# Expert rows through a padded buffer, scattered during attention, instead of a routing table and gathers

## The reference, cut to what matters

```python
xf = layernorm(x).reshape(T, d)                      # T = 2048, d = 256
probs = jax.nn.sigmoid(xf @ gate_w.T)
top_vals, sel = jax.lax.top_k(probs, 2)
weights = top_vals / (top_vals.sum(-1, keepdims=True) + 1e-06)
ranks = (position of each choice among the choices of its expert)
valid = ranks < capacity                             # 320
slot = jnp.where(valid, flat_sel * capacity + ranks, sentinel)
padded = jnp.zeros((sentinel + 1, d)).at[slot].set(x_rep)
h = jax.nn.gelu(einsum('ecd,edf->ecf', padded, w1))
out_padded = einsum('ecf,efd->ecd', h, w2)
out = sum over the two choices of weights * out_padded[slot]
x = x + tanh(g_ffn) * out
```

## Time and profile before

| | us |
|---|---|
| median of 3 runs | 384.05 |
| the profiled execution | 383.44 |
| its span, first to last instruction | 381.7 |
| busy in the span: PE, DVE, ACT, POOL | 315.4, 238.7, 198.0, 243.6 |
| mean granted TensorE clock | 0.933 of 2.4 GHz |

### The profile page before, as it was taken

The page is one execution under the profiler, slowest core; times in us unless marked ns, Lnnn a source line. Parts: engine busy times, 40 slices in busy tenths (PEclk is TensorE's granted clock), DMA queues, the critical chain, the costliest instruction groups (busy, mean ns, idle before and its releaser), DMA issues.

```text
span 381.7 us, 7062 instructions
## 1 busy us (share of the span) xinstructions
PE 315.4 (83%) x2140; PEld 282.1 (74%) x2140; DVE 238.7 (63%) x611; ACT 198.0 (52%) x565; POOL 243.6 (64%) x306
## 2 busy tenths in 40 slices
PE   3989989999999999978402999999999888989500
PEld 2677868988889898867301999999998888879500
DVE  1275968678999898987871476666555535476000
ACT  1073687787876778662510465655645555453100
POOL 6323466755758585655436458888888878787562
PEclk9999999999999999999855799999999999999955
DMA  7794000001011000101106247877776667664332
GB/s 216 231 314 140 2 2 14 29 33 39 27 37 35 27 27 27 41 25 49 42 16 217 64 153 203 209 187 185 200 172 140 145 132 171 172 122 50 41 40 29
DMA packets 31800, 38.23 MB, mean 100 GB/s; under 512 B 4624, under 2 KB 25760, under 8 KB 31776
## 3 DMA queue, kind: packets, MB, share of 16 engines
q1 hardware_dynamic: 23808, 27.44, 22.4%
q0 software_dynamic: 7936, 10.49, 16.8%
q10 hardware_dynamic: 32, 0.02, 0.0%
HBM read 28.10 MB, written 9.83 MB: 99 GB/s over the span
## 4 chain that ended last, share of the span: by engine, by line
POOL 16%; PE 14%; DMA 10%; issue 8%; DVE 2%; ACT 1%; ACTq 0%; POOLq 0%; DVEq 0%
POOL out_dram L551 11%; DMA out_dram<-wqT,rows_to 8%; PE ps_scores L1197 6%; POOL xg L539 4%; PE ps_out L1213 4%; DMA xg<-z_rows,rows_from 2%; PE ps_pT L1181 2%; PE ps_misc L1213 1%; POOL payload L474 0%; ACT wqT L698 0%; PE ps_scores L1115 0%; DVE value_t L963 0%; DVE gden L931 0%; ACT value_t L663 0%; DVE top_i L866 0%
## 5 line engine op out<-in xcount | busy, mean ns | idle before, releaser
L551 POOL DMA_INDIRECT out_dram<-wqT,rows_to x48 | 82.6, 1721 | 24.0 <-issue 11.9
L1197 PE MATMUL ps_scores<-value_t,score_t 128*128 128x320 f32 x384 | 61.1, 316 | 5.8 <-DVE value_t L963 5.8
L539 POOL DMA_INDIRECT xg<-z_rows,rows_from x48 | 49.2, 1025 | 23.5 <-issue 13.4
L1197 PEld LDWEIGHTS ps_scores<-value_t,score_t 128*128 128x128 f32 x384 | 57.8, 192 | 7.1 <-DVE value_t L963 4.7
L1095 PE MATMUL ps_scores<-score_t,xn 128*128 128x512 f32 x192 | 54.4, 426 | 0.0
L1129 PE MATMUL ps_out<-value_t,pT 128*128 128x256 f32 (+1 forms) x384 | 54.0, 291 | 0.4 <-DVE x L840 0.2
L970 DVE TENSOR_TENSOR score_t<-raw,score_t 128x1024 fp32r<-128x1024 f32 x16 | 19.6, 1224 | 51.7 <-ACT score_t L670 33.1
L1129 PEld LDWEIGHTS ps_out<-value_t,pT 128*128 128x128 f32 x384 | 48.7, 193 | 1.2 <-DVE x L840 0.9
L1213 PE MATMUL ps_out<-score_t,value_t 128*128 128x256 f32 x336 | 43.9, 287 | 0.0
L1213 PEld LDWEIGHTS ps_out<-score_t,value_t 128*128 128x128 f32 x336 | 41.0, 191 | 0.9
L1095 PEld LDWEIGHTS ps_scores<-score_t,xn 128*128 128x128 f32 x192 | 36.3, 189 | 6.9
(11 more groups left out here) (171 smaller groups left out, 632.2 us busy)
## 6 DMA issues: line engine op xcount, KB each, us to landing
raw<-in_L_ffn_w_dram SPq DMA_DIRECT2D x32, 512.0 KB
out_dram<-x SPq DMA_DIRECT2D x16, 128.0 KB, 1.7
z_rows<-z SPq DMA_DIRECT2D x16, 128.0 KB, 1.7
x_all<-in_x_dram SPq DMA_DIRECT2D x1, 1536.0 KB, 9.7
wkv_a<-in_L_xattn_Wkv_dram SPq DMA_DIRECT2D x2, 512.0 KB, 7.8
wq_sb<-in_L_xattn_Wq_dram SPq DMA_DIRECT2D x1, 1024.0 KB, 8.8
wo_sb<-in_L_xattn_Wo_dram SPq DMA_DIRECT2D x1, 1024.0 KB, 13.3
xg<-z_rows,rows_from POOLq DMA_INDIRECT x48
```

What stands on the lines that cost most here:

```text
L539: pool.indirect_dma_start(xg[0:SLOTS[k], j, k], None, z2_rows, bass.IndirectOffsetOnAxis(ap=rows_from[0:SLOTS[k], at:at + 1], axis=0)).the ...
L551: pool.indirect_dma_start(out, bass.IndirectOffsetOnAxis(ap=rows_to[0:SLOTS[k], at:at + 1], axis=0), y[0:SLOTS[k], j, k], None, compute_op ...
L1197: op = pe.matmul(ps_scores[:, f, 0:CAPACITY], w1_hl(p, a)[:, c, f * P:(f + 1) * P], x_hl(p, b)[:, c], start=c == 0 and (a, b) == PARTS[0], ...
```

## The change

Rows go from SBUF into a padded buffer in DRAM, `padded`, 2048 rows for each expert, 258 numbers each: the row, its token, its weight. SP fills the first 320 rows of each expert with zeros, with weight 0 and with the spare tokens. Each pair's rows are scattered during attention, two indirect DMAs in each step, four for a pair, to row 2048 x expert + rank. An expert's rows are then fetched by two plain DMAs, and POOL reads token and weight out of what was fetched (`mark`). The table, `z2_rows` and the gathers go; both loops are written out.

```diff
-    z2_rows = nc.dram_tensor("z2_rows", [TOKENS, DIM], F32, kind="Internal").ap()
+    padded = nc.dram_tensor("padded", [EXPERTS * TOKENS, ROW], F32, kind="Internal").ap()
+    padded_init = padded.rearrange("(e s) r -> s e r", e=EXPERTS)
...
-            with engine.Fori(FIRST, LAST) as i:
-                for count, per in counts:
-                    count.enter(i, FIRST, per)
-                for j in range(2):
-                    step(i * 2 + j, j, i)
...
         @block.sync
...
+            sp.wait_ge(empty_ready, 1)
+            for k in range(SLOT_TILES):
+                n = SLOTS[k]
+                sp.dma_start(padded_init[k * P:k * P + n], empty[0:n, k, None, :].to_broadcast([n, EXPERTS, ROW])
+                             ).then_inc(empty_stored, 16)
...
-                t = s - 4
-                if exists(t):
-                    sp.wait_ge(z2_ready, t + 1)
-                    sp.dma_start(z2_rows[bass.ds(t * P, P), :], z2[:, j]).then_inc(z2_stored[j], 16)
...
+            steps(step)
+            for k in range(2):
+                sp.wait_ge(dispatched[k], 64 * PAIRS // 2)
+
+            def fetch(e):
+
+                if exists(e, EXPERTS):
+                    wait(sp, xg_turned, e - 1)
+                    wait(sp, marked, e - 1)
+                    at = e * TOKENS
+                    sp.dma_start(xg[:, e % 2, 0:2], padded[at:at + 2 * P, :].rearrange("(k p) r -> p k r", p=P)
+                                 ).then_inc(fetched[e % 2], 16)
+                    sp.dma_start(xg[0:SLOTS[2], e % 2, 2], padded[at + 2 * P:at + CAPACITY, :]).then_inc(fetched[e % 2], 16)
+
+            fetch(0)
+            fetch(1)
...
                 if exists(e, EXPERTS - 2):
                     sp.wait_ge(w1_low, e + 1)
+                    sp.dma_start(raw1[:, j], w1_load[e + 2]).then_inc(w_loaded[j], 16)
                     sp.wait_ge(w2_low, e + 1)
+                    sp.dma_start(raw2[:, j], w2_load[e + 2]).then_inc(w_loaded[j], 16)
+                if e >= -2:
+                    fetch(e + 4)
...
         @block.gpsimd
...
+            def dispatch(r, k):
+
+                for q in range(2):
+                    pool.indirect_dma_start(padded, bass.IndirectOffsetOnAxis(ap=slot_row[:, r % 2, k, q:q + 1], axis=0),
+                                            z2[:, 2 * (r % 2) + k, q], None).then_inc(dispatched[r % 2], 16)
...
-                    pool.tensor_tensor(payload[:, :, :, :], at_c[:, :, None, :].to_broadcast([P, 4, 3, COLS]),
...
+                if exists(r, PAIRS) and r < PAIRS - 1:
+                    if j == 0:
+                        mark_tokens(r)
+                        pool.wait_ge(slots_ready, r + 1)
+                        if r == 0:
+                            pool.wait_ge(empty_stored, 16 * SLOT_TILES)
+                    dispatch(r, j)
...
-                        done.carry(pool_scratch, minus)
...
-                    done.done(pool.tensor_tensor(l2[:, p, 2:3], l2[:, p, 1:2], mv2[:, p, 0:1], ALU.mult))
-                    pool.tensor_tensor(l2[:, p, 3:4], l2[:, p, 2:3], minus[:, :], ALU.mult).then_inc(ln2_ready, 1)
+                    pool.tensor_scalar(l2[:, p, 2:3], mv2[:, p, 0:1], l2[:, p, 1:2], -1.0, ALU.mult, ALU.mult).then_inc(ln2_ready, 1)
...
+            def mark(e):
+
+                if exists(e, EXPERTS):
+                    pool.wait_ge(fetched[e % 2], 32 * (e // 2 + 1))
+                    done.mark(pool.tensor_scalar(rows_to[:, e], xg[:, e % 2, :, TOKEN], 0.0, None, ALU.add))
+                    pool.tensor_scalar(slot_w[:, e], xg[:, e % 2, :, WEIGHT], 0.0, None, ALU.add).then_inc(marked, 1)
+
+            for e in range(2):
+                mark(e)
+            for e in range(EXPERTS):
                 j, i = e % 2, e // 2
...
-                        pool.indirect_dma_start(xg[0:SLOTS[k], j, k], None, z2_rows,
-                                                bass.IndirectOffsetOnAxis(ap=rows_from[0:SLOTS[k], at:at + 1], axis=0)
-                                                ).then_inc(gathered[j][k], 16)
...
+                mark(e + 2)
+                done.sync()
+                wait(pool, added[(j + 1) % 2], SLOT_TILES * 16 * (i + j))
...
-                    act.activation(z2[:, p], x1[:, p], ACT.Identity, bias=l2[:, p, 3:4],
-                                   scale=l2[:, p, 1:2]).then_inc(z2_ready, 1)
+                    if t >= RING:
+                        act.wait_ge(dispatched[t // 2 % 2], 64 * (t // RING))
+                    act.activation(z2[:, t % RING, :, 0:DIM], x1[:, p, None, :].to_broadcast([P, 2, DIM]), ACT.Identity,
+                                   bias=l2[:, p, 2:3], scale=l2[:, p, 1:2]).then_inc(z2_ready, 1)
...
+                    act.wait_ge(marked, e + 1)
...
+                    if r >= 2:
+                        dve.wait_ge(dispatched[r % 2], 64 * (r // 2))
+                    dve.scalar_tensor_tensor(slot_row[:, r % 2], ef[:, :, :], float(TOKENS), rank[:, :, :], ALU.mult, ALU.add
+                                             ).then_inc(slots_ready, 1)
...
-                        for n in range(4):
-                            op = pe.matmul(ps_table, at_p[:, n], payload[:, n].rearrange("p m c -> p (m c)"),
-                                           start=n == 0, stop=n == 3)
-                        op.then_inc(tabled, 1)
```

More of the change, by code:

```diff
@@ L74, in sync @@
     def sync(self):
[L76 to L90, removed]
+        wait(self.engine, self.sem, self.k)
 def exists(t, n=TILES):
-    return not isinstance(t, int) or 0 <= t < n
-def upto(t, n=TILES):
-    return min(t, n) if isinstance(t, int) else t
+    return 0 <= t < n
 def wait(engine, sem, value):
-    if not isinstance(value, int) or value > 0:
+    if value > 0:
         engine.wait_ge(sem, value)
 def build(nc, x, ctx_in, mask, g_xattn, g_ffn, ln_gamma, ln_beta, wq, wkv, wo, bo, gate_w, w1, w2, out):
-    z2_rows = nc.dram_tensor("z2_rows", [TOKENS, DIM], F32, kind="Internal").ap()
+    padded = nc.dram_tensor("padded", [EXPERTS * TOKENS, ROW], F32, kind="Internal").ap()
+    padded_init = padded.rearrange("(e s) r -> s e r", e=EXPERTS)
     x_rows = x.rearrange("b (t p) d -> (b t) p d", p=P)
@@ L297, in build @@
         w1_high, w1_low, w2_high, w2_low = (sem(n) for n in ("w1_high", "w1_low", "w2_high", "w2_low"))
-        gathered = [[sem(f"gathered{p}_{k}") for k in range(SLOT_TILES)] for p in range(2)]
+        fetched = [sem(f"fetched{k}") for k in range(2)]
+        marked = sem("marked")
         added = [sem(f"added{k}") for k in range(2)]
@@ L337, in steps, with expert_steps @@
                         job(n, *JOBS[n])
-            with engine.Fori(FIRST, LAST) as i:
-                for count, per in counts:
-                    count.enter(i, FIRST, per)
-                for j in range(2):
-                    step(i * 2 + j, j, i)
[L343 to L360, removed]
+        def expert_steps(step):
+            for e in range(-4, EXPERTS):
                 step(e, e % 2, e // 2)
@@ L651, in step @@
                     op.then_inc(exped1, 1)
-            steps(act, step, job=job, jobs_after={-1: range(N_FIRST, N_KEYS + 4), 0: JOBS_AFTER[0]})
+            steps(step, job=job, jobs_after={-1: range(N_FIRST, N_KEYS + 4), 0: JOBS_AFTER[0]})
             act.wait_ge(gated, TILES)
@@ L866, in step @@
                         link.mark(dve.max_index(top_i[:, k], top[:, k], prob[:, k]))
-                if place:
-                    link.sync()
-                    link.mark(dve.scalar_tensor_tensor(over2[:, :, :], rank[:, :, :], float(2 * P), over1[:, :, :], ALU.is_ge, ALU.add))
-                    link.mark(dve.scalar_tensor_tensor(slot_b[:, :, :], ef[:, :, :], float(SLOT_TILES), invalid[:, :, :], ALU.mult, ALU.add))
                 if exists(t1):
@@ L891, in step @@
                     link.sync()
-                    link.mark(dve.scalar_tensor_tensor(slot_p[:, :, :], over2[:, :, :], -float(P), rank[:, :, :], ALU.mult, ALU.add))
-                    link.mark(dve.tensor_tensor(slot_c[:, :, :], slot_b[:, :, :], over2[:, :, :], ALU.add))
-                if place and late:
-                    place_columns()
-                    place_rows()
                 if route:
@@ L919, in step @@
                                       ALU.subtract).then_inc(centred, 1)
-                if route:
-                    link.sync()
-                    link.mark(dve.tensor_scalar(wgt_h[:, :, :], vals[:, :, :, 1], 0.0, None, ALU.add))
                 if exists(t):
@@ L925, in step @@
                     dve.tensor_reduce(row_low[:, 8:HEADS], src[1], AX.X, ALU.min).then_inc(low_ready, 1)
-                if route:
-                    link.sync()
-                    link.mark(dve.tensor_tensor(vals[:, :, :, 2], vals[:, :, :, 1], wgt_h[:, :, :], ALU.subtract))
                 if begin:
@@ L931, in step @@
                     link.mark(dve.tensor_scalar(gden[:, :, :], gexp[:, :, :], 1.0, None, ALU.add))
-                if place and not late:
```

(5 more changed lines are left out.)

240 lines of the change are left out of this document (80 added, 160 removed).

## The result

The changed kernel takes 456.16 us (median of 4 runs, 454.11 to 458.68) where the kernel before takes 383.89 on the same chip: 1.189 times as long, interval 1.183 to 1.196. The forecast was 373.7. The profiled execution has a span of 454.3 us against 381.7. In all that follows a median counts every execution of a kernel, while a ratio and its interval leave out those more than 1.5% above the kernel's fastest (there are such in runs 1, 4, 6 and 7).

What follows compares the result with a forecast made beforehand. PE was taken to bound attention and early experts, POOL the later experts. Expert 0 ends 3.5 us earlier at 221.6, expert 13 121.9 later; two scatter chains (14.4) and a 12.2 tail give span 371.4, median 373.7 us, range 364 to 384.

Steps and rivals of the forecast that it cites:

- Price: nothing: Attention: four scatters per pair fit on POOL, 14.8 of 16.6 us, costing nothing while each stays below about 1.35 us.
- half of the scatters falls into POOL's waiting time: Attention: half of the scatters' 5.2 us per pair falls into the 3.74 us POOL waits in every second step.
- a loop of three experts: Expert stage: weights queue behind fetch and mark, so three experts take 19.65 + 8.66 us, 9.43 us each; chance 0.43.
- rival (a): Expert stage: weights come in time, PE bounds at 8.66 us per expert, 9.3 us earlier, 364.4 us; chance 0.17.
- The scatter, taken at 1.0 us: Attention: a scatter without accumulation takes 1.0 us on POOL, between the gather's 0.96 and the scatter-add's 1.63.
- (c): Attention and handover: a plain scatter costs a scatter-add's 1.63 us, +8.6 us, 382.3 us, counted as same; chance 0.12.
- (d): Attention: DVE holds each dispatch to 1.91 us, so POOL bounds, +11.5 us, +2.1 in the handover: 387.3 us; chance 0.13.
- z2's width: Attention: ScalarE's z2 write, twice as wide, costs 0.2 us more in about five steps, +1.0 us (ends 0 and +3).
- The filling of the buffer: Before attention's end: SP's three DMAs write 5.28 MB in 17 us, over by 55 us, costing nothing.
- The handover: Attention to experts: PE's row transposes start near 204 to 205 us, a gain of 2.5 us, bounds -5 and +1.
- The loops: Both loops become straight code; PE shows no gap at a turn, so this counts for nothing.
- rival (b): Expert stage: a longer loop, 9.90 us per expert as before the change, +6.8 us, 380.5 us; chance 0.15.

Runs made afterwards that it cites:

- run 1: The changed kernel with six z2 tiles instead of four and a dispatched semaphore for each of three pairs: 396.09 us, ratio 1.030.
- run 4: The kernel before with only its two loops written out: 383.21 us, ratio 0.999.
- run 6: The changed kernel, still four z2 tiles, with one semaphore for each tile's scatters and the token marked one tile at a time: 408.11 us.
- run 7: The kernel of run 1 with POOL marking expert e+3 instead of e+2, the fetch left in place: 384.68 us, ratio 0.998.
- run 3: The changed kernel with six z2 tiles and SP fetching rows of expert e+3 instead of e+4: 368.63 us, ratio 0.963.
- run 8: The kernel of run 3 with each dispatch also scattered into a second, unread buffer, eight scatters per pair: 401.03 us, ratio 1.050.

## Why the prediction was wrong

**The step that failed** is the one on attention that ends in "Price: nothing". It counted ScalarE's z2 write at its new width and POOL's scatters at their durations, and said what queues behind the scatters on POOL. It never asked who waits for them. The diff adds, ahead of the z2 write, a wait on `dispatched`; that wait was costed neither in the sum nor in a rival. It is 60 us (runs 1 and 3). It could have been read: the scatters of a pair's second tile are issued in the step after ACT's write of the tile that wants their release, and POOL ends a step with 1.9 us of probabilities and the layernorm's constants. My sentence that half of the scatters falls into POOL's waiting time was right (before the cast of xn it waits 3.78 us ahead of the first scatters and 1.18 in the full pairs of run 3) and beside the point.

**The second miss is of size.** The mechanism among the experts was right: weights behind fetch, fetch behind mark, mark behind three scatters, and a loop of three experts. The first scatters of experts three apart stand 31.6, 32.8 and 32.1 us apart, 10.7 us per expert where I reckoned 9.43. Terms: from the fetch's issue to weights in use I took 6.0 us (7.75 to 13.75) and it is 7.64 in the expert shown (7.6 in the mean of eleven experts, 6.75 to 8.84); the marks I took at 0.5 us, and in the row above they end 1.06 us after the third scatter; from the weights to PE 5.9 was taken and 5.64 measured. These give (28.3 + 1.6 + 0.6 - 0.3) / 3 = 10.1. Of the last 0.6 a part is PE itself: its first product takes 352 ns a piece here and 315 in run 3: right behind the wait shown above, from 315.40 to 320.70 us, the granted clock is 0.68. In sum the queue costs 26.8 us; my forecast had 9.3 for it, as the distance to rival (a). I also named the mark as the one wait ahead of the weights; run 7 shows a second right behind it, PE's turn.

**What held.** Measured where both causes are mended (run 3):
- The scatter, taken at 1.0 us, is 1.03 in the mean there and 1.06 after the change; 0.3 us lie between two.
- POOL has room for four scatters in a pair. Run 8 tests the sum: 9.55 + 0.5 + 8 x 1.31 = 20.5 per pair, 20.2 to 20.5 measured. Rivals (c) and (d) did not happen: the scatters stayed between 0.96 and 1.27 us in the full pairs.
- PE in attention: 16.7 to 16.8 us a pair, where the earlier trace rows has 16.86 and I had 16.6 (with z2's 0.2 us, which that figure left out, my own terms give 16.8); z2's width costs 0.2 us as taken (0.88 in the median for 0.67).
- The filling of the buffer costs nothing, as taken, but by luck: I had it start at 38 us, run at 314 GB/s and be over by 55. It starts at 25.24, the DMA engines move 160 to 204 GB/s between 50 and 58 us, and they quieten only about 60; the first store of x1 is issued at 60.89, in time.
- The handover: slot_row is there at 190.7, earlier than the 192.1 reckoned, but POOL is still at the scatters of the pair before until 191.7, which I had not counted, so the last four begin at 192.38 as reckoned (192.4). They take 5.5 us (to 197.85) where I had 6.8, since only the first was held up; 1.6 us to landing, as taken; PE's transposes start at 202.47, forecast near 204 to 205.
- The loops: nothing (run 4).
- Without its queue the expert stage is rival (a), PE at 8.66 us, full all the time. The first scatters of the experts stand (335.94 - 221.97) / 13 = 8.77 us apart up to the fourteenth, and 7.9 and 7.7 us for the last two, where PE is through. Rival (a) had 364.4 us for a span of 362.1 (371.4 - 9.3); run 3 has a span of 365.6. Of the 3.5, the way to the last expert's scatters has 1.6 (they start at 351.48 where (a) has 335.5 + 14.4 = 349.9) and what lies behind it 1.9 (14.1 us for 12.2). One sign that I had named for "wrong" is there all the same: the scatter-adds are still chained landing to start (30.4 us of waiting, 14 times), while PE is full.

Taken away alone from the changed kernel, the two causes give 60.1 and 26.8 us, together 86.9; taken away at once they give 87.5 (456.16 - 368.63), so nothing of the 72 us lost against the kernel before is left over.

Some sums of the prediction are off without moving it by more than 0.3 us: the handover's terms add up to 203.6 and not 203.9, those of the weights (7.8 + 1.9 + 3.9) to 13.6 and not 13.75, and the +6.8 of rival (b) is 13 x 9.90 less 121.9, not 13 x 0.47, which is 6.1.

The range ended at 384, below rival (d) with its 387.3 and its chance of 0.13, and nothing listed went beyond (d), since every way to be slower that I had listed went through POOL's load. The error behind the error is that the list of rivals was made from engines' loads, not from the waits that the diff adds. That "slower" came out does not bear rival (d) out.

## What to carry to other kernels

Go through every wait that a diff adds, and for each ask at which step of its own engine the signalling instruction stands; a release that is counted by pairs is only as early as its last member, and one step of pipeline offset cost more here than everything the change had won. A ring is to be judged at the shortest steps of the pipeline too: with a release for each tile the full pairs were nearly as short as with the larger ring, and 8.5 us were lost in the tail. In a queue that issues in order, put the transfer whose condition comes late behind those that are free to go: moving one `fetch` by one place was worth 27 us.

## What the runs showed of the hardware that was not expected

- POOL's scatter is stretched beside certain DVE instructions, and DVE's busy share doesn't tell which. In the full pairs of attention it took 0.96 to 1.27 us, with DVE busy for 13.7 of 16.7 us (run 3). In the handover it took up to 1.93, and DVE's order of time shows what was beside it: the rest of the weights, `tensor_tensor` of 128x1024 with two operands in SBUF. POOL's and DVE's rows there, in the changed kernel:

```profile
252.07 1.45 POOL L417 DMA_INDIRECT padded<-z,slot_row  x1 [0.78 <-DVE slot_row L780]
252.56 1.22 DVE L872 TENSOR_TENSOR score_t<-raw,score_t 128x1024 fp32r<-128x1024 f32 x1
253.69 1.22 DVE L875 TENSOR_TENSOR score_t<-raw,score_t 128x1024 fp32r<-128x1024 f32 x1
253.82 1.93 POOL L417 DMA_INDIRECT padded<-z,slot_row  x1 [0.30 <-issue]
...
256.05 0.96 POOL L417 DMA_INDIRECT padded<-z,slot_row  x1 [0.30 <-issue]
```

The scatter at 256.05, with DVE's last such instruction over (253.69 + 1.22), takes 0.96 again. The same holds for POOL's mark of 128 x 3 numbers: 0.22 to 0.26 us alone, 1.38 in the second chain above, where DVE makes casts and rests of `wkv_a` from 299.69 to 301.78. The Trainium skill ("SBUF — State Buffer", "SBUF: two separate sides") says that a DVE instruction with two inputs in SBUF takes the pair of ports from a POOL instruction that reads SBUF, for a whole instruction. That is narrower than my prediction put it. The rows agree that such instructions stretch the scatter, which reads its row numbers from SBUF, and the same section's report that `tensor_tensor` didn't hold up a DMA of POOL's does not hold for this scatter: 1.93 us for 0.96. That the lock lasts for a whole instruction isn't borne out by the first two rows: the scatter of 252.07 ends at 253.52 beside the DVE instruction of 252.56, which takes its usual 1.22 us. Rival (d) had its chance from DVE's busy share; what counted was which instructions stand beside the scatter.

- 1.38 MB issued in four pieces, the rows and the weights of an expert, is in use 6.75 to 8.84 us after the first issue in eleven experts of the changed kernel, 7.6 in the mean; at the plateau of 350 GB/s that I read off the data alone would take 3.9.
